# A one-core attention and expert kernel: attended values, window reads and key copies in another order, and token classes from a code of both indices

## The reference

```python
x = x + conv_ref(ln_c(x), ...)            # layer norm over the 64 channels first
#   q, k, v = 1x1 convolutions, 8 heads of 32
#   attention inside windows of 8 x 8 positions (64 keys), softmax over the keys
#   local_out = 3x3 convolution of v, + b_local
#   out = 1x1 convolution of (attention + local_out), + b_out
t = t + ffn_ref(ln_t(t), ...)             # layer norm again, on the sum
#   logits = t @ Wg + bg; the two largest of 8 experts; softmax over these two
#   out = sum over the two of weight * (gelu(t @ W1[e] + b1[e]) @ W2[e] + b2[e])
```

## Time and profile before

| What | Value |
|---|---|
| median of three runs | 476.1 us (476.08 to 476.41) |
| the profiled execution's own time | 476.03 us |
| its span, first to last instruction | 474.2 us |
| PE busy | 412.1 us (87%) |
| DVE busy | 372.1 us (78%) |
| ACT busy | 341.3 us (72%) |
| POOL busy | 300.3 us (63%) |
| mean granted TensorE clock | 0.987 |

### The profile page before, as it was taken

One profiled execution on the slowest core, in us unless ns is written; L12 is line 12 of the kernel. 1 busy time (PEld: TensorE's weight loads), 2 busy tenths in 40 slices (PEclk: granted clock), 3 DMA queues, 4 the chain that ended last, 5 costly groups with the idle time before them and its releaser, 6 DMA issues.

```text
span 474.2 us, 12547 instructions
## 1 busy us (share of the span) xinstructions
PE 412.1 (87%) x3921; PEld 278.0 (59%) x3921; DVE 372.1 (78%) x1288; ACT 341.3 (72%) x919; POOL 300.3 (63%) x386
## 2 busy tenths in 40 slices
PE   8898888698989879869878868878899999999995
PEld 7353344344444435434434434424799999999995
DVE  4577898757699799799799799898886687877632
ACT  2464787669697697587687675442798899989884
POOL 4232443654744776866866775844777777777775
PEclk9998999999999999999999999989999999999999
DMA  9918500000000000000000000102432222222320
GB/s 211 219 46 172 119 1 2 1 1 1 2 1 2 6 20 18 12 19 18 11 21 13 13 29 20 41 23 56 99 97 73 75 58 55 57 73 72 77 54 0
DMA packets 36168, 22.42 MB, mean 47 GB/s; under 512 B 13648, under 2 KB 33855, under 8 KB 36104
## 3 DMA queue, kind: packets, MB, share of 16 engines
q1 hardware_dynamic: 30264, 14.70, 14.3%
q0 software_dynamic: 4960, 6.45, 4.1%
q10 hardware_dynamic: 880, 0.48, 0.6%
HBM read 13.07 MB, written 9.27 MB: 47 GB/s over the span
## 4 chain that ended last, share of the span: by engine, by line
PE 44%; DVE 28%; issue 13%; POOL 8%; ACT 5%; DMA 2%; DVEq 0%; POOLq 0%; ACTq 0%
PE bank L1629 15%; PE bank L1615 8%; PE bank L1509 7%; DVE mx L1151 5%; PE bank L1458 4%; DVE sm L1159 4%; POOL pn L641 2%; ACT aa L790 2%; DVE sc L1154 2%; POOL hl L551 2%; DVE st L1183 2%; PE bank L1477 2%; DVE xn L1031 1%; POOL out L658 1%; DVE rowb L1180 1%
## 5 line engine op out<-in xcount | busy, mean ns | idle before, releaser
L641 POOL TENSOR_TENSOR pn<-pe_,rs 128x512 f32<-128x512 f32 x64 | 67.0, 1047 | 103.4 <-DVE rs L1162 98.2
L1458 PE MATMUL bank<-aa,bd 64*64 64x256 f32 x512 | 69.9, 389 | 14.2 <-ACT aa L790 6.8
L618 POOL DMA_INDIRECT rows_hbm<-rowb,posu x64 | 65.4, 1022 | 23.3 <-issue 16.8
L658 POOL DMA_INDIRECT out<-bt,zs x63 | 63.3, 1005 | 20.1 <-issue 15.2
L1461 PE MATMUL bank<-pt,bt 64*64 64x256 f32 x512 | 69.9, 390 | 0.9 <-ACT zs L752 0.9
L781 ACT ACTIVATE pe_<-sc 128x512 f32<-128x512 f32 x64 | 40.5, 632 | 35.0 <-DVE sc L1154 33.3
L752 ACT COPY zs<-bank 128x512 f32<-128x512 f32 x64 | 37.2, 582 | 32.6 <-PE bank L1461 32.6
L1458 PEld LDWEIGHTS bank<-aa,bd 64*64 64x64 f32 x512 | 33.2, 133 | 42.9 <-issue 17.6
L1151 DVE TENSOR_REDUCE mx<-bank 128x8 f32<-128x512 f32 x64 | 43.6, 682 | 17.3 <-PE bank L1458 17.2
L1154 DVE TENSOR_TENSOR sc<-bank,mx 128x512 f32<-128x512 f32 x64 | 44.3, 691 | 2.2
L1274 DVE SCALAR_TENSOR_TENSOR bt<-bank,zs 128x64 f32<-128x64 f32 x91 | 25.5, 280 | 24.9 <-PE bank L1629 23.4
(11 more groups left out here) (296 smaller groups left out, 1078.2 us busy)
## 6 DMA issues: line engine op xcount, KB each, us to landing
zs<-rows_hbm SPq DMA_DIRECT2D x91, 66.0 KB, 1.9
wloc<-in_L_conv_w_local SPq DMA_DIRECT2D x2, 1152.0 KB, 9.4
rows_hbm<-zrow SPq DMA_DIRECT2D x1, 1914.0 KB, 14.0
x_sb<-in_x SPq DMA_DIRECT2D x3, 512.0 KB, 10.7
wloc<-in_L_ffn_W SPq DMA_DIRECT2D x2, 512.0 KB, 6.5
rows_hbm<-rowb,posu POOLq DMA_INDIRECT x64, 2.4
out<-bt,zs POOLq DMA_INDIRECT x63, 2.3
wrec<-in_w2b SPq DMA_DIRECT2D x1, 520.0 KB, 5.2
```

The source lines that it names most:

```text
L618: nc.gpsimd.indirect_dma_start(out=rows_hbm, out_offset=bass.IndirectOffsetOnAxis(ap=posu[:, t:t + 1], axis=0), in_=rowb[:, t], in_offset= ...
L641: nc.gpsimd.tensor_tensor(pn[:, v % 2, :].rearrange("p (h j) -> p h j", h=HEADS), pe_[:, v % 2], rs[:, v % 2].unsqueeze(2).broadcast_to([P ...
L658: nc.gpsimd.indirect_dma_start(out=out, out_offset=bass.IndirectOffsetOnAxis(ap=idx_j, axis=0), in_=ob[:, j % LANES], in_offset=None, boun ...
L1458: scored = nc.tensor.matmul(dots[v % 2][same, w * 2 * P:(w + 1) * 2 * P], xq[same, t % 2, 2 * v + w], aa[same, t % 2, :, j0:j0 + WT], star ...
```

## The change

It reorders work on three engines, and writes some small steps in another way.

- PE: the attended values of a group move from slot 3 to slot 0 of the next step, behind the swap (`attended`). The window read moves from behind the nine taps into them, after the fourth (`taps`). For `b < LATE` the gate products move from the end of slot 0 (plan entry 10) to slot 1, ahead of the transposes of `hl` (entry 11).
- ACT: the copy of the first `aa` of a slot comes ahead of the exponential, the second stays behind it. The read into `ys` moves with the attended values, from slot 3 to slot 0 of the next step. For `b < LATE` only `xn2` is computed from the row, and one copy writes the `row16` of the group's four tiles from it, behind a wait of ACT on itself.
- POOL: each normalising step comes ahead of the slot's `pn`.
- DVE: the class is `8 * low + high`, compared with a constant table of the same code; `low` and `high` are reductions of the two indices (uint32); the cast of the indices, and that of the places, are gone.

```diff
-STEADY = dict(..., gate=10, ...
+STEADY = dict(..., gate=11, ...
...
# POOL, body
                     if real(t):
                         if real(nn):
                             before_normalise(nn, u)
+                            normalise(nn, u)
                         wait(pool, rs_ready, at(t, TG, v + 1))
                         wait(pool, pt_done, at(t, TG, v - 1))
                         nc.gpsimd.tensor_tensor(pn[...], pe_[:, v % 2], rs[...], ALU.mult).then_inc(pn_ready, 1)
-                        if real(nn):
-                            normalise(nn, u)
...
# ACT, token_halves
-                    ins = nc.scalar.activation(row16[:, t, 0:C], x1[:, t], ACT.Identity, ...)
                     if b < LATE:
                         ins = nc.scalar.activation(xn2[:, g % 2, t % TG], x1[:, t], ACT.Identity, ...)
+                    else:
+                        ins = nc.scalar.activation(row16[:, t, 0:C], x1[:, t], ACT.Identity, ...)
                     if t % TG == TG - 1:
+                        if b < LATE:
+                            ins.then_inc(half2_ready, 1)
+                            act.wait_ge(half2_ready, g + 1)
+                            ins = nc.scalar.copy(row16[:, t - TG + 1:t + 1, 0:C], xn2[:, g % 2])
                         ins.then_inc(high2_ready, 1)
...
# ACT, body: keys_out is the former loop body, for one head pair
+                    if u in (2, 3) and real(nxt):
+                        keys_out(nxt, 2 * (u - 2))
                     ... the exponential of the slot ...
                     if u in (2, 3) and real(nxt):
-                        for pr in (2 * (u - 2), 2 * (u - 2) + 1):
+                        keys_out(nxt, 2 * (u - 2) + 1)
...
-                    prv = sh(g, -1)
-                    if u == TG - 1 and real(prv):
+                    prv = sh(g, -2)
+                    if u == 0 and real(prv):
                         wait(act, att_done, at(prv, 1, 1))
                         wait(act, yt_done, at(prv, 1, -1))
                         nc.scalar.activation(ys[:, prv % 2, :], attb[:], ACT.Identity, ...).then_inc(y_ready, 1)
...
# DVE, classes
-                    rstep(nc.vector.tensor_copy(first2[:, :, 0:n].rearrange("p k t -> p t k"), topi[:, 0:n, 0:2]))
-                    rlink(nc.vector.tensor_tensor(fall, top[:, 0:n, 1], top[:, 0:n, 0], ALU.subtract))
-                    rstep(nc.vector.tensor_tensor(tied, one, two, ALU.subtract))
-                    rstep(nc.vector.tensor_tensor(low, one, two, ALU.min))
-                    rstep(nc.vector.tensor_tensor(high, one, two, ALU.max))
+                    both = topi[:, 0:n, 0:2]
+                    rstep(nc.vector.tensor_reduce(low, both, axis=AX.X, op=ALU.min))
+                    rstep(nc.vector.tensor_reduce(high, both, axis=AX.X, op=ALU.max))
+                    rstep(nc.vector.tensor_tensor(tied, topi[:, 0:n, 0], topi[:, 0:n, 1], ALU.is_gt))
+                    rstep(nc.vector.tensor_tensor(fall, top[:, 0:n, 1], top[:, 0:n, 0], ALU.subtract))
                 if part == 1:
-                    rstep(nc.vector.scalar_tensor_tensor(tied, tied, 0.0, fall, ALU.is_gt, ALU.mult))
-                    rlink(nc.vector.tensor_scalar(c0, low, -1.0, 2.0 * E - 3.0, ALU.mult, ALU.add))
+                    rstep(nc.vector.tensor_tensor(tied, tied, fall, ALU.mult))
+                    rlink(nc.vector.scalar_tensor_tensor(c2, low, float(E), high, ALU.mult, ALU.add))
                     wait(dve, tanh_ready, b)
                     nc.vector.scalar_tensor_tensor(signed, tied, 2.0, fall, ...).then_inc(gap_ready, 1)
-                    rlink(nc.vector.tensor_tensor(c1, c0, low, ALU.mult))
-                    rlink(nc.vector.scalar_tensor_tensor(c2, c1, 0.5, high, ALU.mult, ALU.add))
...
# DVE, positions
-                rlink(nc.vector.reduce_sum(pos[:, 0:n], pr_[:, 0:n], axis=AX.X))
-                nc.vector.tensor_copy(posu[:, tiles], pos[:, 0:n]).then_inc(pos_ready, 1)
+                    nc.vector.tensor_reduce(posu[:, tiles], pr_[:, 0:n], axis=AX.X, op=ALU.add).then_inc(pos_ready, 1)
...
# PE, body
+                    if u == 0 and real(prv2):
+                        attended(prv2)
                     if u == 1:
+                        for b, k in due("gate", g, u):
+                            gate_logits(b, g, u)
                         ... four transposes of hl ...
                         if real(prv):
-                            ... nine taps ...
+                            taps(prv, 0, 4)
+                        if real(nxt):
+                            ... wait for xsp; the window read into turn[XT] ...
+                        if real(prv):
+                            taps(prv, 4, TAPS)
...
-                        if real(prv):            # at u == 3
-                            ... attended values, waiting for the four zs copies ...
...
-    cst[:, 0] = np.arange(1, CLS + 1)
+    cst[:, 0] = lo * E + hi
```

More of the change, by code:

```diff
@@ L687, in token_halves @@
                         wait(act, norm2_ready, g - 1)
-                    ins = nc.scalar.activation(row16[:, t, 0:C], x1[:, t], ACT.Identity, scale=rstd[:, t:t + 1], bias=nm[:, t:t + 1])
                     if b < LATE:
@@ L995, in positions @@
                 rlink(nc.vector.tensor_tensor(pr_[:, 0:n], pr_[:, 0:n], oh[:, 0:n], ALU.mult))
-                rlink(nc.vector.reduce_sum(pos[:, 0:n], pr_[:, 0:n], axis=AX.X))
-                nc.vector.tensor_copy(posu[:, tiles], pos[:, 0:n]).then_inc(pos_ready, 1)
+                with nc.allow_low_precision(reason="one term of each sum is not zero, and it is a whole number below 2 ** 24"):
+                    nc.vector.tensor_reduce(posu[:, tiles], pr_[:, 0:n], axis=AX.X, op=ALU.add).then_inc(pos_ready, 1)
             def token_norm(b, part):
@@ L1466, in scores_and_values, with taps, attended @@
                     valued.then_inc(z_done, 1)
+            def taps(prv, lo, hi):
+                if lo == 0:
+                    wait(pe, y_ready, at(prv, 1, 0))
+                    if is_step(prv, 0):
+                        pe.wait_ge(cv_in, 16)
+                for k in range(lo, hi):
+                    rhs = xsp[:, prv % 3, :, k // 3:k // 3 + HI, 1 + k % 3:1 + k % 3 + WI]
+                    last = nc.tensor.matmul(attb[:], cv[:, k].rearrange("p a c -> p (a c)"), rhs,
+                                            start=(k == 0), stop=False, skip_group_check=True)
+                if hi == TAPS:
+                    last.then_inc(conv_done, 1)
+            def attended(prv):
+                wait(pe, z_ready, at(prv, TG, TG))
+                for k in range(2):
+                    for hf in range(2):
+                        pr = 2 * hf + k
+                        last = nc.tensor.matmul(attb[hf * C:(hf + 1) * C, :], wvo[:, pr], zs[:, prv % 2, :, pr, :],
+                                                start=False, stop=(k == 1), skip_group_check=True)
+                last.then_inc(att_done, 1)
             def transposed(g, u):
@@ L1502, in body @@
                         if real(prv):
-                            wait(pe, y_ready, at(prv, 1, 0))
-                            if is_step(prv, 0):
-                                pe.wait_ge(cv_in, 16)
-                            for k in range(TAPS):
-                                rhs = xsp[:, prv % 3, :, k // 3:k // 3 + HI, 1 + k % 3:1 + k % 3 + WI]
-                                last = nc.tensor.matmul(attb[:], cv[:, k].rearrange("p a c -> p (a c)"), rhs,
-                                                        start=(k == 0), stop=False, skip_group_check=True)
-                            last.then_inc(conv_done, 1)
+                            taps(prv, 0, 4)
+                        if real(nxt):
+                            wait(pe, xsp_ready, at(nxt, 1, 1))
+                            if real(sh(g, -3)):
+                                wait(pe, x1_ready, at(sh(g, -3), 2, 2))
+                            window_read(g)
+                            nc.tensor.matmul(turn[XT][:], both16[:].rearrange("p k c -> p (k c)"), xsp[:, nxt % 3, :, 1:1 + HI, 2:2 + WI],
+                                             start=True, stop=True).then_inc(xt_done, 1)
+                        if real(prv):
+                            taps(prv, 4, TAPS)
                         for b, k in due("ranks", g, u):
@@ L1568, in body @@
                         conv_weights(u)
-                    if u == 1 and real(nxt):
-                        wait(pe, xsp_ready, at(nxt, 1, 1))
-                        if real(sh(g, -3)):
-                            wait(pe, x1_ready, at(sh(g, -3), 2, 2))
-                        window_read(g)
-                        nc.tensor.matmul(turn[XT][:], both16[:].rearrange("p k c -> p (k c)"), xsp[:, nxt % 3, :, 1:1 + HI, 2:2 + WI],
-                                         start=True, stop=True).then_inc(xt_done, 1)
                     for b, k in due("turned", g, u):
```

32 lines of the change are left out of this document (12 added, 20 removed).

## The result

| | median, us | runs | lowest to highest |
|---|---|---|---|
| before | 476.25 | 4 | 476.08 to 477.56 |
| after | 469.12 | 4 | 466.88 to 471.68 |

The ratio is 0.986 (95% interval 0.982 to 0.991): the change makes the kernel 7 us faster, where 12 were forecast. The profiled execution took 466.88 us and is the fastest of its four; its span is 465.1 us at a mean granted clock of 0.976, where before had 474.2 at 0.987.

What follows compares the result with a forecast made beforehand. Waits between engines with fixed orders were taken to bound attention, no engine being full. Eight groups 8.4, five early groups 2.5 and the last choices 1.2 make 12.1 us off 476.1: 464 us, range 456 to 473.

Steps and rivals of the forecast that it cites:

- the case given 0.2: ACT holds up slot 1, giving 471, or the clock falls once a pair, giving 470; together chance 0.2.
- The pair: Two successive attention groups, A and B, first scores to first scores: 36.11 us before, forecast 34.0, about 1.0 a group.
- the first rival: Gaps before first scores lower PE's clock: once a pair 470 (within a shared 0.2), every group 484 (slower than now: 0.07).
- Five early groups, 2.5: Attention groups before any choice of experts: half the gain taken, 2.5 us.
- Eight groups, 8.4: Attention groups running alongside the choice of experts: 8.4 us gained in all.
- The last choices, 1.2: DVE's final chain: shorter classes for the last two batches save 0.6 us each, 1.2 together.
- The attended values leave this place: Slot 3 to next first scores: where key copies end last, PE just waits instead; each next slot grows by 1.9 us.
- The early read, 1.17 a pair: Window read five taps earlier shortens DVE's wait in B, bringing the next first scores 1.17 us sooner.
- The key copies, 0.53 a group: Slot 3: one of two key copies ahead of the exponential shortens the chain to the next first scores by 0.53 us.
- The gate products, 1.15 in B: First slot of B: moving these products to the next slot removes their 1.15 us wait for `xs2`.
- First to second slot: Attended values add 1.9 us per step, less covered waits: A 2.89 to 4.0, B 3.56 to 4.3; stated as 2.0 longer.
- ACT as the bound: Slot 1: ACT delays the window read by 1.35 us, half the `hl` wait stays: 471; chance 0.2, milder clock case included.

Runs made afterwards that it cites:

- gap_filled: The changed kernel with six unused products on PE behind each group's last key product, before the next first scores: 464.93 us, ratio 0.978 to the kernel before.
- copies_first: The changed kernel with both key copies of slot 3 ahead of that slot's exponential on ACT: 457.28 us, ratio 0.963 to the kernel before.
- back_and_first: The changed kernel with the attended values back in slot 3 and both slot 3 key copies ahead of the exponential: 455.66 us, ratio 0.956.
- late_old_keys: The changed kernel with attended values back in slot 3, late window read, and both key copies behind the exponential again: 454.03 us, ratio 0.953.
- late_old_rows: The changed kernel with attended values back in slot 3, late window read, and ACT computing both token rows from `x1` again: 453.33 us, ratio 0.954.
- after_again: The changed kernel measured and profiled once more with nothing edited: 470.4 us, ratio 0.989 to the kernel before.
- pool_alone: The kernel before with only POOL's new order, each normalising step ahead of the slot's multiplication: 463.8 us, ratio 0.973.

## Why the prediction was right, and what it missed

The direction held, and 469 lies in the range, just above the 459 to 468 that was held likeliest: it is the case given 0.2, "the clock's milder case included". Point by point:

- **The pair was right by its steps.** 33.43 against 34.0; five of the eight steps lie within 0.1 of their forecast, B0 to B1 and B3 to A0 came out 0.4 and 0.5 shorter, B1 to B2 0.2 longer. PE's waits went as said, DVE's for the window read too, and the wait for `xsp` at the window read in A measured 0.60, where 0.5 was taken. Part of this is luck: POOL's order alone makes 2.23 of the 2.68 us won in the pair, where the sum had 2.17 of 2.1 and the other terms cancelled. They nearly did, but two of them, the early read and the key copies, did not measure what was put on them when they were undone in other kernels (below).
- **The step that failed is the clock behind the new gap.** The forecast took it as kept, since "gaps of 1 to 2 us inside attention left the clock at 1.00". What came is the first rival in its milder form, which had it decide "if the gaps before first scores pass 2.4 us in all groups". No such point shows in these traces: of four gaps of 2.35 or 2.36 us one cost the clock, one of 1.99 did, one of 2.68 did not and the like one of 2.67 did. The kernel before had already shown as much: PE's wait of 1.98 us for `hl` is followed there by 0.73 and 0.84, while the prediction took the stretch of 0.63 for the only one.

```profile
40.69 0.40 PE L1499 MATMUL bank<-ident,hl 128*128 128x128 f16 x4 [1.98 <-POOL hl L551]
```

```profile
40.00:44.00 4.00, 3.31 (x13) 1.35 (x14) 1.94 (x4) 1.28 (x3) 1.67 (x3) 0.73 0.98 200
```

  What it took is measured: 470.4 to 464.9 with the gap filled and the pair unchanged, 5.5 us, near the "6 of my 12 us" of that rival; one loss measured 1.6 us, where it had 1.5. That the totals agree is chance: in both profiles only one of the four pairs paid, and the rest was lost in the early groups and at the last one.
- **Five early groups, 2.5.** 0.1 after, 3.1 with the gap filled. The half was a fair size; with the gaps unfilled, those of 1.99 and 3.19 us took it by the clock.
- **Eight groups, 8.4.** 6.3 after, 7.9 with the gap filled.
- **The last choices, 1.2.** The classes themselves came out as priced. Their run on DVE after, from the first reduction to the one-hot compare:

```profile
322.99 0.17 DVE L961 TENSOR_REDUCE pair<-topi 128x8 f32<-128x16 uint32 x1
...
323.80 0.38 DVE L976 TENSOR_TENSOR oh<-cid,cst_sb 128x224 f16<-128x224 f32 x1
```

  That is 0.81 us, before 1.41, and the other run in the last chain is 0.81 too: 0.6 each. But the stretch from the last group's first scores to the end got 0.8 longer. "The last two groups get nothing" was too good: the last group's gap is 4.61 us, before 1.94, and the clock behind it is 0.52; even gap_filled has 3.28 there and 0.84 and 0.74 behind it. The gap itself counts to the eight groups; into the last stretch falls the step behind it, 6.62 us where before had 2.89, since the attended values now stand in it and run at the lower clock.
- **"The attended values leave this place, but where the copies end last, PE merely waits in their stead."** This was true and had its price in the sum (1.9 in each next slot, less the waits it covers). What the text did not say is that this makes the move a loss: 9 us alone and 14.7 within the change. With both copies of slot 3 first it costs less: copies_first and back_and_first lie at 0.963 and 0.956 of before. And POOL's order by itself earns the 12 us forecast for the whole.
- **The early read, 1.17 a pair.** Not confirmed. With the attended values back, reading late is as fast or faster (453.1 against 455.7), and its pair is 1.2 shorter; whether it earned its 1.17 in the change as it stands wasn't tried.
- **The key copies, 0.53 a group.** With the attended values back and the late read, undoing the split makes the pair 0.2 longer (31.89 in late_old_keys, 31.71 without), where 1.06 was put on it. Whether the split earned more in the change as it stands wasn't tried; a second copy ahead did (copies_first, 13 us with what the clock gave back).
- **What was priced at nothing:** ACT's rows were nothing (late_old_rows). DVE's shorter steps inside attention cannot be told apart.
- **The gate products, 1.15 in B.** PE's wait for `xs2` is gone but for one case; what this move earns by itself has no run.
- **Two sums do not come out.** First to second slot the terms make the pair 1.9 longer, not 2.0. For ACT as the bound, 1.35 in both groups instead of 0.5 and nothing, and half the `hl` wait, is 0.85 + 1.35 + 1.08 = 3.3 off the 2.1 won in a pair, so a loss and not "0.3 instead of 1.0". Neither enters the 464.

The lock of the Trainium skill (SBUF — State Buffer, Who interferes with whom) was weighed too: reductions free of it, two-input steps not. The trace after agrees; shortest, median and longest ns of single lines on DVE:

```profile
L961 DVE TENSOR_REDUCE pair<-topi x8: 119/170/172, 134.6 to 323.0; 128x8 f32<-128x16 uint32 x8
...
L999 DVE TENSOR_REDUCE posu<-pr_ x8: 386/386/386, 152.3 to 326.9; 128x8 uint32<-128x224 f32 x8
...
L963 DVE TENSOR_TENSOR gs<-topi x8: 160/278/1123, 134.8 to 323.2; 128x8 f32<-128x8 uint32 x8
```

Neither reduction is ever stretched; the comparison of two index columns beside them grows from 160 to 1123 ns. The other rule of the Trainium skill, that pauses between bursts re-throttle TensorE again and again (TensorE: Matmul & The Clock Gate, HAM oscillation), was taken to put the time near 484; the Trainium skill has it for pauses that are long enough, a condition that the prediction left out. The traces agree with it in part: the clock fell behind 4 of the 14 gaps at first scores of one profile, not behind all.

## What to carry to other kernels

Work that stands where its engine must wait anyway costs nothing there; moved elsewhere, it may have to be paid for, and the bare wait it leaves may cost TensorE's clock besides. A bundle of reorderings can hold a gain and a loss that nearly cancel, so try each move by itself on the kernel before and take each back from the kernel after: here two lines of POOL's order earned more than the whole. When equal runs scatter more than they used to, read the granted clock behind each idle gap; a few idle products in the gap tell at once what it costs.

## What the hardware showed that I had not expected

Equal gaps in equal code had unequal results within one execution: 2.35 us ahead of 167 us left the clock at 1.00, 2.35 ahead of 200 brought it to 0.59. In both profiles of the kernel it was the third of the four equal gaps that did (200.61 here, 206.06 in after_again). A short wait can do it as well: in pool_alone the 1.17 us for `zs` stands ahead of attended values that then took 3.42 us, where one pair later the same wait was followed by 1.94, as before:

```profile
199.66 1.94 PE L1552 MATMUL bank<-zs,wvo 128*64 128x512 f32 x8 [1.17 <-ACT zs L751]
```

In both places a wait of 0.7 to 0.9 us for `aa` stands 2 us ahead. The length of a gap alone does not decide it; what does was not settled here.
